# A graph network on one core: layer 1's weighted messages stay in their PSUM bank, and the sum scan and the first messages change places in the step

## The chip, the cores and the metric

One Trainium2 chip, one of its cores. The metric is the device time of one launch in microseconds (us). The kernel before took 4339.46 us, the median of 3 runs (4338.24 to 4342.36).

## What is computed

Two layers over a graph of 12500 nodes and 212500 edges, whose edges are sorted by destination. Each layer is followed by a residual sum and a layer norm. Layer 0 takes the maximum over a node's edges of a small network. The change lies in layer 1:

```python
x = h[src]; y = h[dst]
c = w_comp[etype]                                   # 16 coefficients per edge
xb = einsum('ei,bio->ebo', x, weight)
msg = einsum('eb,ebo->eo', c, xb)
x_hat = x @ A1_w.T + A1_b
y_hat = y @ A2_w.T + A2_b + rel_emb[etype]
a = tanh(relu(sum(x_hat * y_hat, -1) / sqrt(32)))
nei = segment_sum(a[:, None] * msg, dst)
```

`a * msg` are the weighted messages. A segmented scan along the sorted edges sums them, and the row of a node's last edge holds its sum.

## The kernel before, in words

The edges are cut into 4 streams, and each of 104 steps takes 512 edges of every stream: a tile is 128 partitions (4 streams by 32 features) by 512 edges. Every engine has its own program and works through it in order; semaphores tie them together. The order inside a step is written by hand in one function per engine, each called `step1` for layer 1. `run_steps` writes out the first 12 steps of layer 1, then a loop of 22 rounds with 4 steps each, then 4 more steps.

In step s of layer 1 the engines do the following.

- GpSimd (`gathers1`) fetches the source rows of step s+2 or so by indirect DMA, 128 rows per gather, at L691. Most steps need 15 gathers; the sixteenth tile is picked by matmuls with one-hot matrices (`hot_rows`, L1589). There are two buffers `xg`. A few gathers wait for `coef_done`.
- TensorE (`step1`, L1608) turns the gathered rows of the next step (`source_turn`, L1578 and, for the picked tile, L1575), forms 16 coefficient tiles (`coef`, L1513), each into one of the banks 2, 3 and 6 as `C_BANK` gives them, sums the score (`score_sum`, L1530), and adds up the messages in bank 7 in four parts (`messages`, L1522), of eight matmul records each. A coefficient waits until the product that read its bank before is done: `C_FREE[n]` is the number of products that must be. Coefficient 9 goes to bank 2, which coefficient 6 used before it, so `C_FREE[9]` is 7, products 0 to 6.
- VectorE (`step1`, L1300) multiplies each coefficient tile with the sources (`product`, L1254, eight buffers), and between the products it weighs the messages of the step before (`weigh`, L1262), scans them (`sum_scan`, L1269), scans the destination rows of the next step (`spread_scan`, L1138), adds and multiplies for the score (`find_query`, L1238; `find_score`, L1245), masks and adds the picked tile (L1285, L1293) and compares types (`one_hot`, L1189). Product 8 overwrites the buffer of product 0, so it waits for messages 0.
- ScalarE copies the turned sources (`x4_copy`, L874) and the composed coefficients out of PSUM, and forms the attention (`attend`, L879).
- SP's queue loads, in this order for a step: indices, types, spread rows, `keep` (waits for the scan four steps before) and the one-hot matrix (L573).

Before the change the weighted messages are the tile `wmsg`, a part of `hid` in SBUF. `weigh` reads bank 7 and writes it; `messages(s, 0)`, which overwrites bank 7, waits for `wmsg_ready`; `sum_scan` reads `wmsg` behind product 10.

Of the kernel before, what the change touches and what calls it, by code (L numbers as in the profile page):

```python
# [156 lines left out]
def build(nc, t):  # L157
    ctx = ExitStack()
    with ctx:
# [156 lines left out]
        h_cls = h.rearrange("p (c k) f -> p c (k f)", c=CLASSES)  # L316
        comp = sb("comp", [P, 2, 2, LEN], bf16)

        query, score, wmsg = (hid[:, k // 2, k % 2, :] for k in range(3))
        weight = xt  # L320
        node_t = hid[:, 1, 1, :]

        psum = ctx.enter_context(nc.psum_tensor("psum", [P, 8, 512], fp32))
        bank = [psum[:, i, :] for i in range(8)]
        hot_bank = [bank[6 + u][:, 0:PICK * F] for u in range(2)]
        hot_bank1 = bank[5][:, 0:PICK * F]
        lane_v = lane[:, 0:HOT_COLS].rearrange("p (s t) -> p s t", t=HOT)
# [602 lines left out]
        def _(dve):  # L930
# [365 lines left out]
            def products(s, a, b):  # L1296
                for n in range(a, b):
                    product(s, n)

            def step1(s):  # L1300
                behind, ahead, later = s.plus(-1), s.plus(1), s.plus(2)
                if has_pick(ahead):
                    mask_hot(ahead)
                product(s, 0)
                if has_pick(ahead):
                    add_hot(ahead)
                products(s, 1, 5)
                if behind.exists():
                    weigh(behind)
                products(s, 5, 7)  # L1310
                if ahead.exists():
                    spread_scan(1, ahead, 4)
                product(s, 7)
                if ahead.exists():
                    find_query(ahead)
                products(s, 8, 11)
                if behind.exists():
                    sum_scan(behind)
                products(s, 11, 14)
                if later.exists():  # L1320
                    one_hot(later)
                if has_pick(later):
                    find_lane(later)
                products(s, 14, 16)
                if ahead.exists():
                    find_score(ahead)
# [49 lines left out]
        def _(pe):  # L1376
# [139 lines left out]
            def messages(s, k):  # L1516

                wait_step(pe, s, prod_ready, each=SLOTS, more=(k + 1) * STREAMS - SLOTS)
                if k == 0:
                    wait_step(pe, s, wmsg_ready, lag=1)  # L1520
                for g in range(STREAMS):
                    last_ = pe.matmul(bank[7][F * g:F * g + F, :], basis[:, k, :],  # L1522
                                      prod[:, (k * STREAMS + g) % G_BUFS, :], start=k == 0, stop=k == KCH - 1,
# [84 lines left out]
            def step1(s):  # L1608
# [23 lines left out]
                coef(s, 8)  # L1632
                if turn:
                    source_turn(ahead, 2)
                messages(s, 0)
                coef(s, 9)
                if turn:
                    source_turn(ahead, 3)
                coef(s, 10)
                messages(s, 1)  # L1640
                if pick:
# [160 lines left out]
```

## Time and profile before

| | |
|---|---|
| median of 3 runs | 4339.46 us |
| the profiled execution | 4343.61 us |
| its span | 4341.8 us |
| its mean granted TensorE clock | 0.956 |
| TensorE matmul, busy | 3907.0 us |
| VectorE, busy | 3122.2 us |
| GpSimd, busy | 3217.8 us |
| ScalarE, busy | 903.0 us |

A profile is one execution. Its own time is a little over its span, the time from the first instruction to the last. A row of the timeline gives the start in us, the duration, the engine, the line, the operation, what is written and read, how many instructions follow one another, and in brackets how long the engine was idle before and what ended it. PE is TensorE, DVE is VectorE, POOL is GpSimd. Buffers share names: the products and the turned sources are parts of `late`, `wmsg`, the query and the score are parts of `hid`. Ends of matmuls are modelled.

### The profile page before, as it was taken

The numbers are of one execution on the slowest core, as the hardware profiler recorded it, in microseconds if no ns is written. First come the engines' busy times: TensorE is split into PE (matmuls) and PEld (weight loads), VectorE is DVE, ScalarE is ACT, GpSimd is POOL, SyncE is SP. The second block draws the span as 40 slices with busy tenths as digits, with TensorE's granted clock in tenths as the row PEclk, the third lists the DMA queues.
The fourth block names the chain that finished last, engine by engine and source line by source line (L and its number), as shares of the span: only waits on it lengthen the run. The fifth ranks groups of instructions, "written<-read, shape, count | busy, mean of one in ns | idle before, by whom it ended". The sixth has DMA issues, their size and how long they took to land.

```text
span 4341.8 us, 76892 instructions
## 1 busy us (share of the span) xinstructions
PE 3907.0 (90%) x23347; PEld 1771.7 (41%) x23347; DVE 3122.2 (72%) x5125; ACT 903.0 (21%) x1615; POOL 3217.8 (74%) x3330
## 2 busy tenths in 40 slices
PE   7989999999999999932989999999999999999941
PEld 3444554555455455411533333333333333333311
DVE  7856666666666666526678888888888888888844
ACT  4401111111111111110022222222222222222211
POOL 7767777777777777767777777777777777777745
PEclk9999999999999999965999999999999999999975
DMA  8123333333333333324145555555555555555511
GB/s 340 29 77 105 92 99 98 92 98 98 93 98 98 94 97 98 111 63 76 29 129 140 136 143 137 137 141 136 140 139 135 143 138 138 142 136 138 140 45 32
DMA packets 411406, 494.42 MB, mean 114 GB/s; under 512 B 165363, under 2 KB 314448, under 8 KB 409008
## 3 DMA queue, kind: packets, MB, share of 16 engines
q1 hardware_dynamic: 274800, 278.43, 25.1%
q0 software_dynamic: 106432, 131.97, 13.5%
q10 hardware_dynamic: 29952, 81.80, 5.0%
q14 instruction: 174, 1.43, 0.1%
q8 instruction: 48, 0.79, 0.1%
HBM read 345.09 MB, written 146.77 MB: 113 GB/s over the span
## 4 chain that ended last, share of the span: by engine, by line
PE 38%; DMA 8%; issue 5%; DVE 3%; POOL 1%; DVEq 0%; ACT 0%; POOLq 0%; ACTq 0%
PE psum L1589 8%; PE psum L1513 8%; PE psum L1522 8%; PE psum L1578 4%; DMA xg<-h_dram,src_idx 4%; PE psum L1676 3%; DMA last_rows<-sum_rows,last_i 2%; PE psum L1598 2%; DMA early<-max_rows,last_i 2%; PE psum L1551 1%; PE psum L1530 1%; DVE late L1254 1%; PE psum L1414 1%; PE psum L1575 1%; PE psum L1539 1%
## 5 line engine op out<-in xcount | busy, mean ns | idle before, releaser
L691 POOL DMA_INDIRECT xg<-h_dram,src_idx x1540 | 1502.7, 976 | 481.2 <-DMA xg<-h_dram,src_idx 345.3
L691 POOL DMA_INDIRECT xg<-in_x_dram,src_idx x1392 | 1328.7, 955 | 435.6 <-DMA xg<-in_x_dram,src_idx 306.4
L1254 DVE TENSOR_TENSOR late<-late,psum 128x512 f32<-128x512 f32 x1664 | 1080.0, 681 | 231.0 <-PE psum L1513 191.3
L1428 PE MATMUL psum<-early,late 128*128 128x448 bf16 x5712 | 1131.4, 354 | 9.5 <-DVE late L1051 7.4
L1428 PEld LDWEIGHTS psum<-early,late 128*128 128x128 bf16 x5712 | 545.0, 98 | 628.3 <-issue 115.9
L1513 PE MATMUL psum<-comp,sel 128*128 128x512 bf16 x1664 | 587.1, 384 | 42.1 <-DVE late L1254 41.5
L1522 PE MATMUL psum<-late,basis 128*32 128x512 f32 x3328 | 446.0, 608 | 0.0
L1589 PE MATMUL psum<-x,late 128*128 128x448 bf16 x1344 | 380.6, 353 | 0.0
L1051 DVE TENSOR_TENSOR late<-psum,lane_hot 128x448 f32<-128x448 f32 x272 | 169.7, 624 | 289.1 <-PE psum L1428 275.0
L1159 DVE TENSOR_TENSOR_SCAN scan<-fresh,scan,psum 128x512 f32<-128x512 bf16 x103 | 131.8, 1280 | 326.4 <-PE psum L1474 326.2
L1513 PEld LDWEIGHTS psum<-comp,sel 128*128 128x128 bf16 x1664 | 154.9, 98 | 493.5 <-DVE late L1254 299.3
L874 ACT COPY late<-psum 128x512 f32<-128x512 f32 x416 | 233.8, 587 | 520.8 <-PE psum L1578 307.1
L1032 DVE TENSOR_SCALAR late<-late,class_id 128x384 bf16<-128x384 f32 (+2 forms) x728 | 335.4, 531 | 0.0
L1138 DVE TENSOR_TENSOR_SCAN dt_<-keep,dt_,psum 128x512 f32<-128x512 bf16 x206 | 262.4, 1274 | 46.7 <-PE psum L1404 46.7
L1054 DVE TENSOR_REDUCE xg<-late 128x32 f32<-128x448 f32 x272 | 252.6, 929 | 9.3
L1578 PE MATMUL psum<-ident,xg 128*128 128x128 f32 x1540 | 229.8, 280 | 18.3 <-DMA xg<-h_dram,src_idx 12.8
L831 ACT ACTIVATE hid<-psum,b 128x512 f32<-128x512 f32 x208 | 131.6, 684 | 536.3 <-PE psum L1464 536.3
L1589 PE MATMUL psum<-late 128*128 128x448 bf16 x672 | 236.9, 352 | 0.0
L896 ACT COPY early<-psum 128x512 f32<-128x512 f32 x104 | 60.8, 585 | 822.4 <-PE psum L1414 822.4
L1494 PE MATMUL psum<-ident,early 128*128 128x128 f32 (+1 forms) x56 | 15.6, 434 | 231.1 <-DVE early L1180 119.5
L1578 PEld LDWEIGHTS psum<-ident,xg 128*128 128x128 f32 x1540 | 177.6, 142 | 97.6 <-ACT late L874 39.6
L836 ACT COPY out<-psum 128x512 f32<-128x512 f32 x104 | 61.0, 586 | 743.2 <-PE psum L1414 743.2
(159 smaller groups left out, 4424.7 us busy)
## 6 DMA issues: line engine op xcount, KB each, us to landing
sp_in<-spread SPq DMA_DIRECT2D x208, 256.0 KB, 3.7
late<-type_dram SPq DMA_DIRECT2D x104, 512.0 KB
sum_rows<-early ACTq DMA_DIRECT2D x104, 512.0 KB
spread<-late SPq DMA_DIRECT2D x16, 1664.0 KB
ea<-in_edge_t SPq DMA_DIRECT2D x104, 256.0 KB
keep<-keep_dram SPq DMA_DIRECT2D x832, 32.0 KB
max_rows<-out ACTq DMA_DIRECT2D x104, 256.0 KB, 2.1
xg<-h_dram,src_idx POOLq DMA_INDIRECT x1540
```

Of the source, the lines that this page charges most:

```text
L691: pool.indirect_dma_start(out=out, out_offset=None, in_=table, in_offset=bass.IndirectOffsetOnAxis(ap=index, axis=0), engine_sem=pool_issu ...
L874: act.copy(x4[:, s.slot(2), g, :], bank[g % 2][:, :]).then_inc(x_ready[1], 1)
L1032: last_ = dve.tensor_scalar(class_hot[u][:, tiles, c, :], class_in[:, u, tiles, :], class_id[:, c:c + 1], None, ALU.is_equal)
L1051: dve.tensor_tensor(picks[:, u], hot_bank[u].rearrange("p (h f) -> p h f", f=F), bc(lane_hot[:, t, :], size, 2), ALU.mult).then_inc(hot_re ...
L1054: dve.tensor_reduce(xg0[:, s.slot(PRE), SLOTS - hot_tiles(s) + t, :], picks[:, u].rearrange("p h f -> p f h"), AX.X, ALU.add).then_inc(hot ...
L1138: dve.tensor_tensor_scan(dt_[:, s.slot(2), :], keep[:, s.slot(4), :], bank[b][:, :], before(s, dt_), ALU.mult, ALU.add).then_inc(d_ready[n ...
L1254: dve.tensor_tensor(prod[:, n % G_BUFS, :], x4[:, s.slot(2), g, :], bank[C_BANK[n]][:, :], ALU.mult).then_inc(prod_ready, 1)
L1428: last_ = pe.matmul(hot_bank[tile_slot(s, t)], class_hot[s.slot(2)][:, HOT - hot_tiles(s) + t, c, :], x_parts[:, c, q, :], start=c == 0 an ...
L1513: pe.matmul(bank[C_BANK[n]][:, :], sel[:, (g % 2) * KCH + k, :], comp[:, s.slot(2), g // 2, :], start=True, stop=True).then_inc(coef_done, 1)
L1522: last_ = pe.matmul(bank[7][F * g:F * g + F, :], basis[:, k, :], prod[:, (k * STREAMS + g) % G_BUFS, :], start=k == 0, stop=k == KCH - 1, ...
L1578: last_ = pe.transpose(out[:, j, :], xg[:, s.slot(2), row, :], ident[:, :])
L1589: last_ = pe.matmul(hot_bank1, hot1[:, s.slot(2), c, :], h_parts[q][:, c, :], start=n == 0, stop=n == CLASSES * PARTS - 1)
```

## The change

`wmsg` becomes bank 7 itself. `weigh` reads bank 7 and writes its result over it, and the scan reads it there. The scan moves on VectorE from behind product 10 to behind product 5. The first messages of a step now wait for the scan of the step before in place of its `wmsg_ready`, and TensorE issues them behind coefficient 9 and the last source turn, where they stood behind coefficient 8 and turn 2.

```diff
--- before.py
+++ after.py
@@ -316,12 +316,13 @@
         h_cls = h.rearrange("p (c k) f -> p c (k f)", c=CLASSES)
         comp = sb("comp", [P, 2, 2, LEN], bf16)
 
-        query, score, wmsg = (hid[:, k // 2, k % 2, :] for k in range(3))
+        query, score = (hid[:, 0, k, :] for k in range(2))
         weight = xt
         node_t = hid[:, 1, 1, :]
 
         psum = ctx.enter_context(nc.psum_tensor("psum", [P, 8, 512], fp32))
         bank = [psum[:, i, :] for i in range(8)]
+        wmsg = bank[7]
         hot_bank = [bank[6 + u][:, 0:PICK * F] for u in range(2)]
         hot_bank1 = bank[5][:, 0:PICK * F]
         lane_v = lane[:, 0:HOT_COLS].rearrange("p (s t) -> p s t", t=HOT)
@@ -1307,16 +1308,16 @@
                 products(s, 1, 5)
                 if behind.exists():
                     weigh(behind)
-                products(s, 5, 7)
+                product(s, 5)
+                if behind.exists():
+                    sum_scan(behind)
+                product(s, 6)
                 if ahead.exists():
                     spread_scan(1, ahead, 4)
                 product(s, 7)
                 if ahead.exists():
                     find_query(ahead)
-                products(s, 8, 11)
-                if behind.exists():
-                    sum_scan(behind)
-                products(s, 11, 14)
+                products(s, 8, 14)
                 if later.exists():
                     one_hot(later)
                 if has_pick(later):
@@ -1517,7 +1518,7 @@
 
                 wait_step(pe, s, prod_ready, each=SLOTS, more=(k + 1) * STREAMS - SLOTS)
                 if k == 0:
-                    wait_step(pe, s, wmsg_ready, lag=1)
+                    wait_step(pe, s, scanned[1], lag=1)
                 for g in range(STREAMS):
                     last_ = pe.matmul(bank[7][F * g:F * g + F, :], basis[:, k, :],
                                       prod[:, (k * STREAMS + g) % G_BUFS, :], start=k == 0, stop=k == KCH - 1,
@@ -1632,10 +1633,10 @@
                 coef(s, 8)
                 if turn:
                     source_turn(ahead, 2)
-                messages(s, 0)
                 coef(s, 9)
                 if turn:
                     source_turn(ahead, 3)
+                messages(s, 0)
                 coef(s, 10)
                 messages(s, 1)
                 if pick:
```

## Rows read from the trace of the kernel before

**Rows 1.** The page, part 1: busy time, share of the span, instructions.

```profile
PE 3907.0 (90%) x23347; PEld 1771.7 (41%) x23347; DVE 3122.2 (72%) x5125; ACT 903.0 (21%) x1615; POOL 3217.8 (74%) x3330
```

**Rows 2.** Timeline of TensorE: start, duration, line, idle time before; two score sums.

```profile
2485.87 1.02 PE L1530 MATMUL psum<-hid,ones_blk 128*128 128x512 f32 x2
...
4104.77 1.02 PE L1530 MATMUL psum<-hid,ones_blk 128*128 128x512 f32 x2
```

**Rows 3.** Groups of instructions of GpSimd between the two starts of rows 2.

```profile
L691 POOL DMA_INDIRECT xg<-h_dram,src_idx x1261 | 1230.8, 976 | 389.4 <-DMA xg<-h_dram,src_idx 281.9 <-PE psum L1513 55.4 <-issue 52.0
```

**Rows 4.** Timeline around 2997 us, one gather and the scan it began in.

```profile
2997.33 1.28 DVE L1269 TENSOR_TENSOR_SCAN scan<-keep,scan,hid 128x512 f32<-128x512 bf16 x1
...
2997.55 1.82 POOL L691 DMA_INDIRECT xg<-h_dram,src_idx  x1 [0.30 <-DMA xg<-h_dram,src_idx]
```

**Rows 5.** Groups by form between 2200 and 4100 us, the two scans.

```profile
L1138 DVE TENSOR_TENSOR_SCAN dt_<-keep,dt_,psum 128x512 f32<-128x512 bf16 x99 | 125.9, 1272 | 0.0
L1269 DVE TENSOR_TENSOR_SCAN scan<-keep,scan,hid 128x512 f32<-128x512 bf16 x98 | 125.2, 1277 | 0.0
```

**Rows 6.** Timeline of TensorE in two successive steps.

```profile
3044.97 1.02 PE L1530 MATMUL psum<-hid,ones_blk 128*128 128x512 f32 x2
...
3050.19 1.04 PE L1578 MATMUL psum<-ident,xg 128*128 128x128 f32 x8
3051.07 0.38 PE L1513 MATMUL psum<-comp,sel 128*128 128x512 bf16 x1
3051.47 0.66 PE L1578 MATMUL psum<-ident,xg 128*128 128x128 f32 x4
3052.05 1.06 PE L1522 MATMUL psum<-late,basis 128*32 128x512 f32 x8
3053.05 0.39 PE L1513 MATMUL psum<-comp,sel 128*128 128x512 bf16 x1
3053.28 0.49 PE L1578 MATMUL psum<-ident,xg 128*128 128x128 f32 x3
...
3054.38 1.06 PE L1522 MATMUL psum<-late,basis 128*32 128x512 f32 x8
...
3063.64 1.02 PE L1530 MATMUL psum<-hid,ones_blk 128*128 128x512 f32 x2
...
3069.12 1.09 PE L1578 MATMUL psum<-ident,xg 128*128 128x128 f32 x8
```

**Rows 7.** Timeline of VectorE in the first of these steps.

```profile
3049.13 0.68 DVE L1262 SCALAR_TENSOR_TENSOR hid<-xt,psum 128x512 f32<-128x512 f32 x1
3049.73 1.28 DVE L1254 TENSOR_TENSOR late<-late,psum 128x512 f32<-128x512 f32 x2
3050.93 1.27 DVE L1138 TENSOR_TENSOR_SCAN dt_<-keep,dt_,psum 128x512 f32<-128x512 bf16 x1
3052.12 0.66 DVE L1254 TENSOR_TENSOR late<-late,psum 128x512 f32<-128x512 f32 x1
```

**Rows 8.** Timeline of the step before, at the loop's head, VectorE and TensorE.

```profile
3026.73 0.68 DVE L1254 TENSOR_TENSOR late<-late,psum 128x512 f32<-128x512 f32 x1
...
3027.46 0.39 PE L1513 MATMUL psum<-comp,sel 128*128 128x512 bf16 x1 [0.35 <-DVE late L1254]
...
3031.05 0.68 DVE L1262 SCALAR_TENSOR_TENSOR hid<-xt,psum 128x512 f32<-128x512 f32 x1
...
3035.71 1.07 PE L1522 MATMUL psum<-late,basis 128*32 128x512 f32 x8
```

**Rows 9.** Waits of VectorE: waited for, us in total, times, longest.

```profile
DVE late L1285 <- issue: 62.5, 21, 3.7
```

**Rows 10.** Timeline of TensorE, one long wait near each end of layer 1.

```profile
2261.58 1.93 PE L1578 MATMUL psum<-ident,xg 128*128 128x128 f32 x8 [2.65 <-DMA xg<-h_dram,src_idx]
...
4130.49 1.97 PE L1578 MATMUL psum<-ident,xg 128*128 128x128 f32 x8 [4.31 <-DMA xg<-h_dram,src_idx]
```

**Rows 11.** Busy time by stretch, 4130 to 4136 us; PEclk is third from the end.

```profile
4130.00:4136.00 6.00, 5.51 (x25) 3.17 (x26) 0.23 (x1) 1.76 (x3) 4.47 (x6) 0.53 0.23 51
```

## The prediction

> **What bounds the kernel now.** I began with the page. TensorE is busy for 90% of the span, VectorE for 72%, GpSimd for 74% [rows 1]. All lines of the diff lie in layer 1's loop, so I cut out its 84 like steps, from one score sum to another: 4104.77 - 2485.87 = 1618.9 us [rows 2]. Three engines run close together there, and the question is which of them is late at which point.
>
> GpSimd first. In that stretch it issues 1261 gathers, busy 1230.8 us and idle 389.4 us, together 1620.2 us, the whole stretch [rows 3]. The idle time is about 0.30 us behind each gather. It never rests: over many steps the gathers set today's rate, although TensorE looks fuller.
>
> Why do they take so long? The median gather takes 0.94 us, the mean 0.976 [rows 3]. One of the long ones, 1.82 us, began 0.22 us into the scan at L1269 and ended 0.76 us behind its end [rows 4]. I laid all gathers against all scans: 40 of those that began inside an L1269 scan were stretched so, and all of these ended 0.75 us or so behind it, 20.1 us in sum. Of 102 that began inside an L1138 scan none was. The two scans differ in one operand: L1138 reads its data from PSUM, L1269 from hid in SBUF [rows 5]. 15.3 of the 20.1 us lie in the 84 steps, 4.1 in the first 15 steps. The other stretched gathers overlap the one-hot at L1189, which stays.
>
> TensorE next. In a step where it waits for nothing, score sum to score sum takes 3063.64 - 3044.97 = 18.67 us; in the next, turn 0 starts 5.48 us into the step instead of 5.22, on the last gather [rows 6]. Of the 84 steps 27 are free like the first, 36 wait for a gather, and 21 stand at the loop's head, where VectorE stops for 3.0 us on average (62.5 us, 21 times, no releaser seen) [rows 9]. There TensorE follows VectorE for some coefficients.
>
> **The change, part by part.** I count from the score sum, t = 0 at 3044.97.
>
> *The scan's operand.* weigh and scan keep their number. The scan from PSUM takes 1272 ns against 1277 from SBUF [rows 5]: nothing on VectorE. On GpSimd it gives back the stretches, 15.3 us in the 84 steps, if something else doesn't bind. The Trainium skill speaks against it: VectorE: DVE Perf Modes, "The TRN2 errata", gives a fixed 120 cycles for a PSUM source against 58 for an SBUF one, that is 0.065 us more per scan, 5.5 us over 84 steps, by which the result would be near 4347. The trace does not agree (1272 against 1277 ns), and I go by the trace.
>
> *weigh writes PSUM, in the bank that it reads.* No VectorE row writes PSUM. Bounds: its successor starts 0.60 us behind it today, and the shortest row of 512 elements there lasts 0.66 us where weigh lasts 0.68, so 0.02 gained at most; at worst it costs what a scan does to its successor, 1.19 us, so 0.59 more [rows 7]. I take 0.60, the row of the same form.
>
> *The scan behind product 5.* VectorE reaches weigh at 4.16 and product 5 at 4.76 [rows 7]. Then the scan starts at 5.36 and product 6 at 5.36 + 1.19 = 6.55 (the pitch of L1138) and ends at 7.21 (0.66). Today it ends near 6.0. Queued behind the scan on VectorE are product 6, the spread scan, product 7, the query and products 8 to 10; then VectorE idles for coefficient 11 today, and that idle time takes up the shift, so the later ones don't move. What waits for product 6? Coefficient 9: they share bank 2 (C_FREE[9] = 7).
>
> *TensorE's order.* Today: turn 2 at 6.50, messages 0 at 7.08, coefficient 9 at 8.08, turn 3 at 8.31, messages 1 at 9.41 [rows 6]. A set of four transposes takes 0.44 us before a full-width coefficient (0.88 for the eight of turns 0 and 1), but 0.58 before messages. So TensorE would be ready for coefficient 9 at 6.50 + 0.44 = 6.94. It must wait for product 6 at 7.21, plus 0.06 for the semaphore (a product that ends at 3027.41 lets a coefficient go at 3027.46, others 0.06 to 0.07) [rows 8]: 7.27. From there turn 3 comes 0.23 later, then 1.10 as from turn 3 to messages 1 today, with 1.00 of messages 0 in between: messages 1 at 9.60 instead of 9.41. A free step costs **+0.19**, 18.86 us. Everything behind messages 1 keeps its place. Messages 0 start near 8.28; their new wait, the scan's end at 6.63, is covered, and product 8 at 9.5 finds them done at 9.28.
>
> *The loop's head.* There VectorE is late: weigh starts at 3031.05 and messages 1 at 3035.71 [rows 8]. By the same chain (0.60 + 0.60 + 1.19 + 0.66 + 0.06 + 2.33 = 5.44) messages 1 come at 3036.49: **+0.78**. Before, the lateness was over once messages 0 ran; now product 6 is behind a scan just where TensorE asks for it. Over the 21 heads, each from its own weigh, the mean is +0.70 (four with a short stop pay less).
>
> *The steps bound by gathers.* They fall to 18.86, which is 0.19 less on average, as GpSimd's need is then 1620.2 - 15.3 = 1604.9 us, below TensorE's.
>
> *Sum for the 84 steps:* 27 x 0.19 - 36 x 0.19 + 21 x 0.70 = 5.1 - 6.8 + 14.7 = **+13.0 us**, TensorE-bound at 1631.9.
>
> *Both ends of the layer.* In the first 15 steps GpSimd is last: TensorE waits 2.65 us at 2261.58 [rows 10] and short gather waits follow. Given back: the 4.1 us of stretches there, **-4.0**. At the other end TensorE waits 4.31 us at 4130.49 [rows 10], and then its granted clock is 0.53 for 6 us, between its two levels and mostly at 1.2 GHz [rows 11], which costs some 2.3 us. By then the gathers are 27 us less in arrears (1631.9 - 1604.9), as far as two xg buffers allow, over 10 us; both go: **-6.4**, with the longer step taken off.
>
> *SP, ACT.* SP's keep loads wait for the scan and go out 4.8 us earlier, then the hot load; their readers come steps later. ACT's copies for turns 2 and 3 end before these start. Nothing.
>
> **Total: +13.0 - 4.0 - 6.4 = +2.6 us.** The profiled execution took 4343.61 us (span 4341.8), the median of the runs 4339.46; the difference is between executions, so I put the sum on the median: **4342 us**. 0.2% of it, 8.7 us, is what a measurement can tell from no change.
>
> **Rivals.**
> *A, slower: writing weigh's result to its own PSUM bank costs time.* For it: no row shows that write. Against it: reads from PSUM cost nothing extra. The place is the chain weigh, product 5, scan, product 6, coefficient 9, which binds in all 84 steps, so each 0.1 us there is 8.4 us. It decides from (8.7 - 2.6) / 84 = 0.07 us up. With 0.15 us: 2.6 + 12.6 = +15, 4355; the upper bound, 0.59, would give 4392. Chance 0.22.
> *B, faster: product 6 is in time,* since the pieces around it are shorter than I have them, and coefficient 9 waits for nothing. TensorE then saves 0.14 a step (6.94 + 2.33 = 9.27), falls under the gathers' need, and the steps follow GpSimd: -15.3 - 4.0 = -19.3, 4320. For it: GpSimd is today's limit, and the change frees it. Against it: VectorE's pitches are read off rows, and 0.33 us is missing even in a free step, over 0.9 at the heads. The Trainium skill has a rule for B's first half: VectorE: DVE Perf Modes, "Two Vector instructions with no wait between them", says that the second of two SBUF tensor inputs is read through an interface shared with GpSimd. By that rule the trace agrees (40 stretched, 0 at L1138). Chance 0.16.
> *C, it does not do what it says:* gathers stretch as before, from whatever they collide with now that the SP loads are bunched, and absorb part of the waits at coefficient 9. Loop +13, ends nothing: with half absorbed +6.5, 4346. Chance 0.12, three quarters of it within 0.2%.
>
> **How the numbers follow.** The forecast has 0.50; its own spread is the stop at the loop's head (0.3 us a stop, 6 us in 21) and 0.05 us in the chain (4 us): 4334 to 4350. Of it 0.37 is within 0.2%, 0.10 slower, 0.03 faster. Slower: 0.10 + A 0.20 + C 0.03 = 0.33. Faster: 0.03 + B 0.16 = 0.19. Same: 0.37 + 0.02 + 0.09 = 0.48. The range takes in A's 4355 and the upper part of B: 4326 to 4356.
>
> **What would show it.** In the changed profile: the L1269 form's successor reads psum and lasts 1.27 us; no gather that begins in it is stretched; the mean gather falls from 976 to about 964 ns; coefficient 9 begins 7.27 us behind the score sum; free steps last 18.86; heads are 0.7 longer; GpSimd waits for TensorE at last; the 4.31 us wait near the end is gone. A weigh longer than 0.68, or product 5 over 0.60 behind it, speaks for A. Coefficient 9 at 6.94 and steps of about 18.7 to 18.9 bound by gathers speak for B. Stretched gathers inside the new scan speak for C, and if coefficient 9 still comes at 8.08, I have misread the order.

## The result and the profile after

The changed kernel takes **4303.11 us** (median of 4 runs, 4302.11 to 4305.04) where the kernel before takes 4339.51 in the runs beside it: ratio 0.9916, interval 0.9899 to 0.9933. It is 0.84% faster. I had forecast 4342 us, no change; the result lies outside the range, on the faster side.

All results below are ratios to the kernel before on the same chip, and this matters: on some chips the kernel before itself takes 5994 to 6053 us, on the others 4340 to 4346 us. Only the second kind behaves as the profiles of before and after do.

The page, part 1 (compare [rows 1]):

```profile
PE 3879.8 (90%) x23347; PEld 1782.7 (41%) x23347; DVE 3119.3 (73%) x5125; ACT 902.7 (21%) x1615; POOL 3183.5 (74%) x3330
```

GpSimd has 34 us less to do with the same instructions. The 84 steps, from score sum to score sum (compare [rows 2]), in TensorE's timeline:

```profile
2476.12 1.02 PE L1531 MATMUL psum<-hid,ones_blk 128*128 128x512 f32 x2
...
4072.32 1.02 PE L1531 MATMUL psum<-hid,ones_blk 128*128 128x512 f32 x2
```

That is 1596.2 us against 1618.9. The same stretch in the groups of instructions (compare [rows 3]):

```profile
L692 POOL DMA_INDIRECT xg<-h_dram,src_idx x1266 | 1205.5, 952 | 391.9 <-DMA xg<-h_dram,src_idx 282.9 <-issue 69.4 <-PE psum L1514 39.6
```

The mean gather fell from 976 to 952 ns. 1205.5 + 391.9 = 1597.4 us: GpSimd still hardly rests. VectorE's scan and GpSimd's gathers beside it (compare [rows 4, 5]):

```profile
3054.59 1.27 DVE L1270 TENSOR_TENSOR_SCAN scan<-keep,scan,psum 128x512 f32<-128x512 bf16 x1
3055.36 0.94 POOL L692 DMA_INDIRECT xg<-h_dram,src_idx  x1 [0.30 <-DMA xg<-h_dram,src_idx]
```

This gather begins 0.77 us into the scan and takes its 0.94 us. I call a gather well inside a scan when it begins at least 0.10 us behind the scan's start and at least 0.21 us before its end. In the changed kernel 68 gathers are well inside the moved scan and none is stretched; in the kernel before 41 were, and all 41 were stretched.

That is half of what GpSimd got back. Over the 84 steps, what the long gathers take beyond their usual 0.944 us adds up to 40.9 us in the kernel before: 15.3 in the scan, and 25.6 nearly all in gathers that overlap the one-hot of L1189, such as this one:

```profile
3058.68 1.27 POOL L691 DMA_INDIRECT xg<-h_dram,src_idx  x1 [0.31 <-PE psum L1513]
3059.08 0.75 DVE L1189 TENSOR_SCALAR late<-late,row_id 128x2048 bf16<-128x2048 bf16 x1
```

In the changed kernel the sum is 10.8 us, all of it outside the scan. So 15.3 us went with the operand and another 14.8 beside the one-hot, which was not touched: the gathers now meet it at other moments. The prediction had let these stand.

A plain step on TensorE (compare [rows 6]):

```profile
3049.23 1.02 PE L1531 MATMUL psum<-hid,ones_blk 128*128 128x512 f32 x2
...
3055.73 0.66 PE L1579 MATMUL psum<-ident,xg 128*128 128x128 f32 x4
3056.50 0.39 PE L1514 MATMUL psum<-comp,sel 128*128 128x512 bf16 x1
3056.72 0.49 PE L1579 MATMUL psum<-ident,xg 128*128 128x128 f32 x3
3057.14 0.43 PE L1576 MATMUL psum<-ident,xg 128*32 128x128 f32 x8
3057.39 1.04 PE L1523 MATMUL psum<-late,basis 128*32 128x512 f32 x8
3058.36 0.39 PE L1514 MATMUL psum<-comp,sel 128*128 128x512 bf16 x1
3058.68 1.06 PE L1523 MATMUL psum<-late,basis 128*32 128x512 f32 x8
...
3067.95 1.02 PE L1531 MATMUL psum<-hid,ones_blk 128*128 128x512 f32 x2
```

Coefficient 9 begins 7.27 us behind the score sum, as forecast. Messages 1 begin at 9.45, not 9.60, and the step takes 18.72 us, not 18.86. All 63 steps that are not the first of a round take 18.72; before, their mean was 18.89. VectorE in the same step (compare [rows 7]):

```profile
3053.39 0.69 DVE L1263 SCALAR_TENSOR_TENSOR psum<-xt,psum 128x512 f32<-128x512 f32 x1
3053.99 0.68 DVE L1255 TENSOR_TENSOR late<-late,psum 128x512 f32<-128x512 f32 x1
3054.59 1.27 DVE L1270 TENSOR_TENSOR_SCAN scan<-keep,scan,psum 128x512 f32<-128x512 bf16 x1
3055.78 0.66 DVE L1255 TENSOR_TENSOR late<-late,psum 128x512 f32<-128x512 f32 x1
3056.36 1.27 DVE L1139 TENSOR_TENSOR_SCAN dt_<-keep,dt_,psum 128x512 f32<-128x512 bf16 x1
```

`weigh`, which now writes PSUM, takes 0.69 us and its successor comes 0.60 behind it; product 6 begins at 6.55. This is the working of the prediction to the hundredth.

Another thing that I had not foreseen stands in VectorE's waits (compare [rows 9]; waited for, us in total, times, longest):

```profile
DVE late L1286 <- issue: 49.5, 21, 3.7
```

The stop at the head of a round fell from 2.98 to 2.36 us, and the head steps from 20.43 to 19.85 us, where I had 21.13. At both ends of the layer the waits of TensorE for gathers shrank: to 1.7 us in the first steps (2187 to 2486 us; 4.7 before), and to nothing in the last ones, where before it stood 4.31 us [rows 10].

Where the 39.8 us of the two spans lie:

| us | before | after | difference | forecast |
|---|---|---|---|---|
| start to the first score sum of layer 1 | 2191.8 | 2187.4 | -4.4 | 0 |
| the first 16 steps | 294.0 | 288.7 | -5.3 | -4.0 |
| 63 plain steps | 63 x 18.89 | 63 x 18.72 | -10.5 | |
| 21 head steps | 21 x 20.43 | 21 x 19.85 | -12.2 | |
| these 84 steps | 1618.9 | 1596.2 | -22.7 | +13.0 |
| the last three score sums | 60.0 | 51.8 | -8.2 | -6.4 |
| the rest | 177.0 | 177.9 | +0.9 | 0 |

The first row is no part of the change: over eight profiled executions on chips of this kind its time lies between 2187.0 and 2192.7 us, with no order in it.

### The profile page after: what moved, and what is told of

The parts are those of the page before. It is cut to its first block, busy times and chain, and to the rows that moved or that the text cites. A ratio compares the mean times of both kernels' runs of the same rounds, so it can differ in the third digit from the quotient of the medians.

```text
span 4302.0 us, 76892 instructions
## 1 busy us (share of the span) xinstructions
PE 3879.8 (90%) x23347; PEld 1782.7 (41%) x23347; DVE 3119.3 (73%) x5125; ACT 902.7 (21%) x1615; POOL 3183.5 (74%) x3330
## 4 chain that ended last, share of the span: by engine, by line
PE 30%; DVE 10%; issue 8%; DMA 5%; DVEq 1%; POOL 0%; ACT 0%; POOLq 0%; ACTq 0%
PE psum L1590 9%; PE psum L1523 6%; DVE late L1255 6%; PE psum L1514 6%; PE psum L1677 3%; DMA last_rows<-sum_rows,last_i 2%; PE psum L1599 2%; DMA early<-max_rows,last_i 2%; DVE psum L1263 1%; PE psum L1415 1%; DVEq L437 1%; PE psum L1579 1%; DVE xg L1294 1%; DMA xg<-h_dram,src_idx 1%; PE psum L1576 1%
## 5 line engine op out<-in xcount | busy, mean ns | idle before, releaser
L692 POOL DMA_INDIRECT xg<-h_dram,src_idx x1540 | 1466.5, 952 | 482.1 <-DMA xg<-h_dram,src_idx 346.0
L1255 DVE TENSOR_TENSOR late<-late,psum 128x512 f32<-128x512 f32 x1664 | 1085.8, 680 | 213.6 <-PE psum L1514 202.0
L1052 DVE TENSOR_TENSOR late<-psum,lane_hot 128x448 f32<-128x448 f32 x272 | 169.9, 625 | 286.8 <-PE psum L1429 273.0
L1139 DVE TENSOR_TENSOR_SCAN dt_<-keep,dt_,psum 128x512 f32<-128x512 bf16 x206 | 262.5, 1274 | 45.8 <-PE psum L1405 45.8
L1495 PE MATMUL psum<-ident,early 128*128 128x128 f32 (+1 forms) x56 | 15.6, 435 | 232.2 <-DVE early L1181 119.9
```

The costliest lines, as they stand in the source:

```text
L692: pool.indirect_dma_start(out=out, out_offset=None, in_=table, in_offset=bass.IndirectOffsetOnAxis(ap=index, axis=0), engine_sem=pool_issu ...
L1052: dve.tensor_tensor(picks[:, u], hot_bank[u].rearrange("p (h f) -> p h f", f=F), bc(lane_hot[:, t, :], size, 2), ALU.mult).then_inc(hot_re ...
L1139: dve.tensor_tensor_scan(dt_[:, s.slot(2), :], keep[:, s.slot(4), :], bank[b][:, :], before(s, dt_), ALU.mult, ALU.add).then_inc(d_ready[n ...
L1255: dve.tensor_tensor(prod[:, n % G_BUFS, :], x4[:, s.slot(2), g, :], bank[C_BANK[n]][:, :], ALU.mult).then_inc(prod_ready, 1)
```

## The experiments

There were two theories. **G**: the scan's operand in SBUF stretches the gathers, they set the rate, and the place of the messages (PSUM) makes the gain. **R**: the two new orders make it. Later a third question came up: what sets the stop at the head of a round.

### Both orders, messages in SBUF (e13)

```diff
-        query, score = (hid[:, 0, k, :] for k in range(2))
+        query, score, wmsg = (hid[:, k // 2, k % 2, :] for k in range(3))
...
-        wmsg = bank[7]
...
-                    wait_step(pe, s, scanned[1], lag=1)
+                    wait_step(pe, s, wmsg_ready, lag=1)
```

> Both new orders, the weighted messages in SBUF, the ordinary data. On a chip of some 4340 us: theory R (the two orders make the gain; e12 kept TensorE's 18.72 us a plain step with 25 of 87 gathers inside the scan stretched) expects the changed kernel's ratio, 0.990 to 0.993, plain steps of 18.72 us and a head step of 19.7 to 20.1. Theory G (the place of the messages makes it, through the gathers) expects 0.996 or more and plain steps over 18.8 us. On a chip of some 6000 us both expect 0.992 to 0.995, as in e8.

Measured: 4319.1 us, ratio 0.9948 (0.9931 to 0.9965), between the two theories. So the orders are worth 0.5% and the place, on top of them, about 0.3% (the two intervals just touch, but this kernel's fastest run, 4316.9 us, lies above the changed kernel's slowest, 4305.0); by the spans 22.7 us (4341.8 to 4319.1, of which 4.8 lie ahead of layer 1) and 17.1 (to 4302.0). A gather in GpSimd's timeline, and TensorE's waits from 2440 to 4040 us:

```profile
3098.41 1.84 POOL L691 DMA_INDIRECT xg<-h_dram,src_idx  x1 [0.30 <-DMA xg<-h_dram,src_idx]
```

```profile
PE psum L1513 <- DVE late L1254: 27.3, 51, 1.1
PE psum L1578 <- DMA xg<-h_dram,src_idx: 1.5, 2, 0.8
```

31 gathers are stretched in the scan again, by 19.0 us in sum, among them all 28 that are well inside it; with the place moved to PSUM (the changed kernel) it is 0 of 68. G's mechanism is shown. But in the 84 steps the stretches hardly bind: TensorE waits 1.5 us for gathers and its plain steps take 18.73 us. The reason is again in GpSimd's rows: over the 84 steps the long gathers lose 12.1 us in the scan, little less than the 15.3 before, but 5.2 us outside it, where it was 25.6. So part of what the orders gain comes through the gathers too, by the one-hot and not by the scan. Stretch by stretch, the place is worth 5.0 us of the 84 steps (1601.2 against 1596.2), 5.7 of the first 16 (294.4 against 288.7) and 7.8 of the last three (59.6 against 51.8). The orders are worth 17.7 us in the 84 steps, and within 0.4 us nothing in the first 16 and the last three.

### Messages in PSUM, TensorE's old order (e14)

```diff
                 if turn:
                     source_turn(ahead, 2)
+                messages(s, 0)
                 coef(s, 9)
                 if turn:
                     source_turn(ahead, 3)
-                messages(s, 0)
```

> Messages in PSUM, the scan early, messages 0 ahead of coefficient 9 as before. From e13 (both orders with SBUF: 0.9948) the place is worth 0.4% and the orders 0.5%. If TensorE's own move gives the orders' part, by sparing product 6's semaphore a wait, this kernel has plain steps of 18.8 to 19.0 us and a ratio of 0.995 to 1.000. If the move is neutral or costs 0.19 us a step, as my prediction had it, plain steps are 18.6 us or less and the ratio is 0.989 to 0.991.

Measured: 4314.19 us (4302.88 to 4315.70), ratio 0.9926 (0.9910 to 0.9943), in neither of the two ranges expected, the interval overlapping the changed kernel's. The profiled execution is the fastest, 4302.88. Messages 0, turn 3 and messages 1 in a plain step, from the score sum at 3049.10:

```profile
3056.18 1.06 PE L1523 MATMUL psum<-late,basis 128*32 128x512 f32 x8
3057.40 0.49 PE L1579 MATMUL psum<-ident,xg 128*128 128x128 f32 x3 [0.16 <-issue]
3057.82 0.43 PE L1576 MATMUL psum<-ident,xg 128*32 128x128 f32 x8
3058.50 1.07 PE L1523 MATMUL psum<-late,basis 128*32 128x512 f32 x8
```

Messages 1 at 9.40 and 18.67 us a plain step, against 9.45 and 18.72. TensorE's own move therefore costs 0.05 us a step, as a mechanism of the sign that I had forecast and a quarter of its size. It brings no gain in this profile: the 84 steps take 1594.3 us, the least of the kernels with a stop at the head. Whether it pays in the runs at 4313 to 4316 us stays open; I have no profile of one.

### TensorE's order alone (e15)

```diff
-                messages(s, 0)
                 coef(s, 9)
                 if turn:
                     source_turn(ahead, 3)
+                messages(s, 0)
```

> Messages in SBUF, the scan behind product 10 as before, messages 0 behind coefficient 9. Gathers under the scan: if the early scan's place among the gathers is what lets them run ahead, the lead stays at 5 gathers as before, over 35 are stretched inside the scan, and the ratio is 0.998 to 1.003. If TensorE's order alone makes the orders' part, 0.994 to 0.996.

Measured: 4365.75 us, ratio 1.0044 (1.0027 to 1.0060): slower than before, just outside the first expectation and far from the second. TensorE's waits, 2440 to 4040 us, and GpSimd's group there:

```profile
PE psum L1578 <- DMA xg<-h_dram,src_idx: 45.7, 54, 1.0
```

```profile
L691 POOL DMA_INDIRECT xg<-h_dram,src_idx x1230 | 1225.6, 996 | 375.8 <-DMA xg<-h_dram,src_idx 275.1 <-issue 72.6 <-PE psum L1513 28.1
```

All 97 gathers well inside the scan are stretched, by 66.7 us; the mean gather takes 996 ns and the plain steps 19.33 us. With the scan at its old place the engines have settled so that a gather begins 0.1 to 0.5 us into nearly every scan. That is the gathers' rate in its pure form: over the 84 steps the gathers lose 22.9 us more than in the kernel before (63.8 against 40.9), and the steps take 21.5 us more. TensorE's move alone costs time; VectorE's move pays in e14 without it, together with PSUM. VectorE's move by itself, with the messages in SBUF, has no run on these chips.

### The changed kernel with VectorE's instructions moved in memory (e16)

```diff
+            for _ in range(64):
+                dve.wait_ge(dve_done, 1)
             run_steps(dve, step1, 4, 3)
```

> The changed kernel with 64 fulfilled waits ahead of VectorE's steps of layer 1, so that every instruction of the steps lies elsewhere in memory. If the layout of the 8 KB pieces sets the heads (e11 and e12, with other instructions ahead of the steps, had heads of 20.9 us at the same stop of 2.0 us): the head steps move off 19.85 us by 0.5 us or more and the time by 10 us or more either way. If only the gathers' lead and the DMAs that meet the loads set them: head steps of 19.6 to 20.1 us and the time within 0.15% of 4303 us.

Measured: 4305.74 us, ratio 0.9904 (0.9888 to 0.9921). VectorE's waits, the line that takes the place of the stop, and TensorE's:

```profile
DVE late L1255 <- remote: 15.0, 21, 0.8
```

```profile
PE psum L1581 <- DMA xg<-h_dram,src_idx: 16.6, 43, 0.9
```

The stop is gone from in front of L1286; 0.7 us of it are left, 21 times, in front of a product. So half of each expectation came true: the head steps moved, by 1.0 us to 18.86, and the time did not. The DMA queue q14, which carries instructions, shows why the stop went: in the 84 steps it moves 117 packets of 8192 bytes in the kernel before, in the changed one and in e11 to e15, and 13 here. The 64 waits took away five loads a round, so those were VectorE's. Yet the time did not move, because now TensorE waits for gathers: the 84 steps take 1586.5 us, 9.7 less, which is 15 gathers of 0.950 and their 0.31 us of idle time (18.9 us) a step; the last three steps pay 6.4 us for gathers that are no longer ahead (58.2 against 51.8), the first 16 pay 3.4, and 3.5 lie ahead of layer 1. **With gathers of this length 1586 us is what GpSimd allows, whatever is done to the heads.**

### The same with layer 0's result set to zero (e11, e12)

```diff
                 link(dve.reciprocal(stat_c[:, :], stat_b[:, :]))
+                if n < CHUNKS:
+                    link(dve.memset(stat_c[:, :], 0.0))
```

e12 has e13's edit too. Both were meant for the chips of 6000 us, and met one of 4342.

> The changed kernel with layer 0's result h set to zero (one memset on VectorE a chunk, in front of layer 1): every gather, one-hot row, product, turn and scan of layer 1 runs as before, on zeros. It asks why the kernel took about 6000 us on the chips of the first three jobs, where TensorE stood some 6 us in each step. Theory P (TensorE is held there for what its data make it draw): on such a chip the 84 steps of layer 1 fall from 28.7 us towards the 19 us of the first profiles, 104 steps by up to 1000 us, and layer 0's steps stay. Theory Q (it is held for its activity, whatever the data, or for its instructions): the time stays within 1% of the changed kernel's. On a chip that takes 4340 us for the kernel before, both expect 4303 us within 5 us.

> The same zeros with both new orders and the weighted messages in SBUF. If the zeros bring the steps of 19 us back (or the chip has them anyway): theory G (the scan's SBUF operand stretches GpSimd's gathers, and they set the rate) expects 0.3% or more over e11 (13 us or more), over 30 stretched gathers inside the scan, and TensorE waiting for gathers in several steps; theory R (the two orders make the whole gain) expects e11's time within 0.15%. If the steps stay at 28 us, both expect no difference, as in e7 and e8.

Measured: 4474.8 us (ratio 1.0305, 1.0288 to 1.0322) and 4474.8 us (1.0311, 1.0293 to 1.0328). Neither theory had that. The plain steps take 18.72 us in both, although in e12 all 25 gathers well inside the scan are stretched, which bears e13 out; the head steps take 28.0 and 26.7. VectorE's waits in e11 (2440 to 4200 us), GpSimd's, and one head:

```profile
DVE late L1288 <- issue: 146.5, 21, 8.6
DVE xg L1296 <- issue: 47.1, 21, 6.3
```

```profile
POOL xg L692 <- ACT early L892: 182.1, 30, 11.1
```

```profile
3050.85 0.75 DVE L1248 SCALAR_TENSOR_TENSOR hid<-psum,a1b,hid 128x512 f32<-128x512 f32 x1
3059.53 0.62 DVE L1288 TENSOR_TENSOR late<-psum,lane_hot 128x448 f32<-128x448 f32 x1 [7.93 <-issue]
```

The extra memsets move VectorE's instructions as e16's waits do, and here it costs: there is a second stop in each round, in front of L1296, of 1.1 us in the second and third head and about 2 us or more in the others. Those two heads take 20.9 us at a first stop of 2.3. The gathers get further ahead with each round, and from the fifth head on, when GpSimd is a whole step ahead and stands for the buffers, the first stop is 7.4 to 8.6 us. That gave the clue to what the stop is.

### What the stop is: DMA packets in front of the instruction load

VectorE's instructions come in DMA packets of 8192 bytes on queue q14 (e16). At each head of a round VectorE goes on 2.0 to 2.4 us behind the start of one such load, in all 105 heads of before, after, e13, e14 and e15 and in the 42 of e11 and e12, however long it stands. The DMA view of the 4 us before a head, in the kernel before (3019.4 to 3023.4 us; packets, MB, share of 16 engines):

```profile
q1 hardware_dynamic: 432, 0.51, 43.6%
q0 software_dynamic: 230, 0.48, 40.6%
q14 instruction: 1, 0.01, 1.0%
```

and in the changed one (3005.3 to 3009.3 us):

```profile
q0 software_dynamic: 127, 0.26, 23.5%
q1 hardware_dynamic: 22, 0.03, 2.2%
```

q1 carries SP's loads. SP's issues before the head at 3023.38 us in the kernel before:

```profile
3011.48 0.35 SPq L654 DMA_DIRECT2D src_idx<-in_src_t  x1
3012.09 0.38 SPq L656 DMA_DIRECT2D late<-type_dram  x1
...
3017.77 1.85 SPq L579 DMA_DIRECT2D keep<-keep_dram  x4
3019.99 0.35 SPq L573 DMA_DIRECT2D late<-hot_dram  x1
```

and before the head at 3009.18 us in the changed one:

```profile
2992.60 0.35 SPq L655 DMA_DIRECT2D src_idx<-in_src_t  x1
2993.20 0.38 SPq L657 DMA_DIRECT2D late<-type_dram  x1
...
2998.76 2.98 SPq L580 DMA_DIRECT2D keep<-keep_dram  x4
3002.12 0.35 SPq L574 DMA_DIRECT2D late<-hot_dram  x1
```

The `keep` load waits for a scan, and the scan is 5.1 us earlier (it starts 5.36 us behind the score sum, where it started 10.42 behind, both medians); the index and type loads wait for gathers, and the gathers are further ahead. So the whole burst goes out earlier and ends earlier. Means over the 21 heads, in us relative to the end of `find_score`, after which VectorE stands (a minus is before it). The burst on q1 ends with the last packet of the run that begins with the one-hot load; "ahead" is how many gathers have begun at a typical head's score sum, counted from 5 in the kernel before:

| kernel | type load issued | one-hot load issued | burst on q1 ends | load before the head's | head's load starts | stop | ahead |
|---|---|---|---|---|---|---|---|
| before | -11.3 | -3.4 | +0.5 | -2.4 | +0.7 | 2.98 | 5 |
| e15, late scan | -11.1 | -2.4 | +0.6 | -2.2 | +0.6 | 2.88 | 5 |
| e13, early scan | -12.4 | -5.4 | -0.6 | -2.8 | +0.4 | 2.53 | 7 |
| e14, early scan | -13.9 | -6.5 | -1.8 | -4.0 | +0.2 | 2.38 | 8 |
| after | -15.6 | -7.2 | -3.0 | -4.2 | +0.2 | 2.36 | 9 |

Over the 105 heads of these five kernels the head's load never starts less than 2.6 us behind the load before it. Where that one starts 3.5 us or more before the end of `find_score` (34 heads, on average 177 DMA packets that start within 3 us of that point) the mean stop is 2.2 us; where it starts within 2.2 us (21 heads, 675 packets) it is 3.4 us. VectorE's new program by itself doesn't make the stop short: in the changed kernel the first and third head, where the bursts still run over the head (to +1.9 and +0.7), have stops of 3.7 and 3.5 us.

The plainest case is in e11 and e12. At 31 of their heads the type load, 512 packets of 1024 bytes, goes out at -2.1 to -1.9 us and runs over the head. The head's load starts at +5.3 to +6.5, and in 30 of the 31 within 0.3 us of the end of the type load's last packet. At the fourth head of e11 the type load goes out at +0.5, behind the start of the head's load, and that stop is 2.1 us; the second stop is the one of 6.3. That traffic holds the load back is shown there. That it does so in the kernel before as well, and that the earlier loads are what shortened the stop from 2.98 to 2.36, is read from timing, head by head; I tried no kernel in which SP's loads alone are held back.

The Trainium skill has the frame for this: Runtime: NRT & Kernel Launch, "Instruction fetch mechanics", says that a sequencer fetches its instructions through a DMA queue of its own, and that a taken branch whose target is not in its window must wait for the fetch. The trace agrees with the second part, 1.9 to 8.6 us a head. On the size, 16 KiB a block by the Trainium skill, VectorE's loads disagree, with 8192 bytes each; the 48 loads on q8, none of them in the loop, are of 16384.

### The chips of 6000 us (e1 to e10, e17, e18)

On these the kernel before takes 5994 to 6053 us. The changed kernel there, the page's part 1 and two rows of VectorE's waits:

```profile
PE 4286.2 (71%) x23079; PEld 1885.4 (31%) x23347; DVE 3143.2 (52%) x5125; ACT 906.2 (15%) x1615; POOL 3170.3 (53%) x3330
```

```profile
DVE late L1255 <- remote: 606.8, 188, 9.3
DVE late L1052 <- remote: 543.2, 88, 17.3
```

VectorE's, ScalarE's and GpSimd's busy times are within 1% of those on the other chips, but VectorE, ScalarE and GpSimd wait, up to 17 us at a time, for releases that the profile puts down to nothing on the core, in layer 0 (L1052) as in layer 1 (L1255); TensorE's granted clock is 0.856 and the steps take 28.7 us. I did not find out why. The edits: e1 and e5 are e13's kernel, e8 too; e2 is e15's; e4, e9 and e18 are e14's; e7 is the changed kernel, e10 is e16's; e6 and e17 are the kernel before with e16's 64 waits; e3 is the kernel before with VectorE's move alone:

```diff
-                products(s, 5, 7)
+                product(s, 5)
+                if behind.exists():
+                    sum_scan(behind)
+                product(s, 6)
...
-                products(s, 8, 11)
-                if behind.exists():
-                    sum_scan(behind)
-                products(s, 11, 14)
+                products(s, 8, 14)
```

> Both moves of the change, but wmsg stays in hid in SBUF and the first messages wait for wmsg_ready as before. Theory G (the scan's SBUF operand stretches gathers, and the gathers set the rate): stretched gathers inside the scan come back, about 40 or more, the mean gather rises to 970 ns or more, the time is 4325 to 4350 us. Theory R (the gain is TensorE's and VectorE's order, the operand does little): 4303 to 4310 us with coefficient 9 at 7.27 us and a plain step of 18.72. For the shorter stop at the loop's head (2.35 us mean in place of 2.98): if it comes from VectorE's order of instructions it stays at 2.3 to 2.5; if it comes from the gathers being ahead it goes back to 2.9 to 3.1.

> Only TensorE's order changes: messages 0 behind coefficient 9 and turn 3. Product 6 is in time then, so coefficient 9 should begin near 6.94 us into a plain step and messages 1 near 9.12, a step of 18.39 us if nothing else binds. Theory G: the gathers set the rate, so the time stays at 4337 to 4342 us. Theory R: 84 steps gain 0.28 each, 4312 to 4318 us. Head stop: 2.9 to 3.1 if VectorE's order sets it, since that order is the old one.

> Only VectorE's order changes: the scan behind product 5, from SBUF, TensorE's order as before. Coefficient 9 comes behind messages 0 at 8.08, where product 6 is long done, so a plain step keeps 18.67. Theory G: stretched gathers as before or more, 4335 to 4350 us. Theory R: the heads alone gain, 4318 to 4325 us. Head stop: 2.3 to 2.5 if VectorE's order sets it, 2.9 to 3.1 if not.

> The change without its TensorE part: in place in PSUM, scan behind product 5, messages 0 behind coefficient 8 and turn 2 as before. A plain step goes from 18.72 back to 18.67 (coefficient 9 at 8.08, no wait for product 6), 63 x -0.05 = -3; at a head messages 0 may wait up to 0.2 us for the scan, but coefficient 9 no longer waits for product 6 (-0.5 to -0.8 a head). Theory G with TensorE as the bound of the changed kernel: 4288 to 4302 us, TensorE's move worth nothing or a loss. If TensorE's move was needed for the gain, 4305 us or more.

> The kernel of e1 once more, since before itself took 6050 us in that job. Theory G (the scan's SBUF operand stretches gathers and the gathers set the rate): with the median of before near 4340 us this one takes 4325 to 4350 us, with 40 or more stretched gathers inside the scan. Theory R (the two orders make the gain): 4303 to 4312 us. Head stop 2.3 to 2.5 us if VectorE's order of instructions or the place of the scan sets it, 2.9 to 3.1 if the gathers' lead does.

> The kernel before with 64 waits that are long fulfilled, once, ahead of VectorE's layer 1 steps: nothing in the loop changes, but its instructions lie elsewhere in memory and in the 8 KB pieces in which the instruction queue loads them. Theory L (where the pieces' borders fall decides how late the load at the loop's head starts): the mean stop at the 21 heads leaves 2.98 us by 0.3 or more and the time moves by 5 to 25 us, either way. Rival (the stop hangs on traffic or on the order inside the loop): stop 2.9 to 3.1, time within 3 us of before.

> The changed kernel itself, beside the runs of before on the same chip. On a chip like that of the first profiles: ratio 0.992. On one where the kernel before takes about 6000 us, as in the two jobs so far: theory R (the new orders of VectorE and TensorE make the gain) expects the ratio of the run with both orders and the messages in SBUF, 0.990 to 0.994; theory G (the SBUF operand stretches GpSimd's gathers and those set the rate) expects clearly less, about 0.985.

> Both new orders, the weighted messages in SBUF as before. Theory R (orders make the gain): within 0.2% of the changed kernel, 0.990 to 0.994 of before. Theory G (the stretched gathers set the rate): at most half of the gain is left, 0.996 or more where the changed kernel has 0.992; over 30 of some 100 gathers inside the scan are stretched again, and TensorE waits for gathers again where it does not in the changed kernel.

> The weighted messages in PSUM and VectorE's new order, but messages 0 ahead of coefficient 9 on TensorE as before. Beside the slow chips (1.022): if TensorE's move is what makes the early scan pay, at least 0.5% slower than the changed kernel on any chip. If on TensorE's ordinary clock the move is worth nothing, as my prediction's term of +0.19 us a step has it, this kernel is as fast as the changed one or up to 0.4% faster (84 steps by 0.19 us are 16 us).

> The changed kernel with 64 waits that are always fulfilled ahead of VectorE's steps of layer 1: they move every later instruction of VectorE by a constant in memory and leave each step as it is. Theory L (where the 8 KB pieces of instructions end sets the stop at the head of a loop): the mean stop at the 21 heads moves off 2.35 us, by 0.3 us or more, and the time by 7 us or more (0.2%). Theory O (the shorter stop comes of the order inside the loop or of gathers that are ahead): the stop stays within 0.2 us and the time within 0.15%.

> The kernel before with the same 64 fulfilled waits: by e16 VectorE should then find its instructions at the head of a loop, and the stop of 2.98 us a head be gone. Theory L (the stops, 21 of them, cost before what after does not pay): the 84 steps fall by the heads' excess, 21 x (20.43 - 18.89) = 32 us, and the kernel is as fast as the changed one. Theory G (the gathers set the rate in the kernel before, whatever the heads do): the steps lose their heads but the plain ones grow, TensorE waits for gathers more than 8.8 us, over 60 gathers inside the scan are stretched, and at most 12 us are gained (ratio 0.997 or more).

> The kernel of e14 again; its runs lay at 4302.9 and at 4313 to 4316 us. Its plain steps of 18.67 us against 18.72 say that TensorE's move costs 0.05 us a step, some 3 us, where the engine sets the rate. If the runs at 4313 to 4316 us are this kernel's usual ones, a profile of one of them shows the 11 us in other steps than the plain ones: at the heads, in steps 4 to 14 or in the last three. If the move is worth nothing, the median is within 0.1% of the changed kernel's 4303 us.

| kernel | ratio there | ratio on the other chips |
|---|---|---|
| changed (e7) | 0.9940 (0.9923 to 0.9956) | 0.9916 |
| changed, moved in memory (e10) | 0.9949 (0.9932 to 0.9965) | 0.9904 |
| both orders, SBUF (e1, e5, e8) | 0.9938, 0.9902, 0.9940 | 0.9948 |
| TensorE's order alone (e2) | 1.0034 (1.0016 to 1.0052) | 1.0044 |
| PSUM, TensorE's old order (e4, e9, e18) | 1.0222, 1.0169, 1.0198 | 0.9926 |
| VectorE's order alone (e3) | 1.0200 (1.0180 to 1.0219) | not run |
| before, moved in memory (e6, e17) | 1.0005, 1.0006 | not run |

What follows: there the place is worth nothing once the scan is early (e7 and e8 are equal, and in neither does a gather begin inside the scan), and the early scan pays only together with TensorE's move (e3 and e4 against e1 and e7), which on the ordinary chip costs 0.05 us a step. Both findings belong to that regime. e10 and e6 asked about a stop that is not what limits there: the 64 waits take the loads away there too (13 packets on q14 in the 84 steps where e7 has 118), and the time stays. e17 was to tell whether the kernel before is set by its gathers even without the stops; it met such a chip, and that stays open.

## Why the prediction was wrong

**What held.** The bound: GpSimd never rests in the kernel before, and the gathers that are stretched in the scan come of its SBUF operand; without the operand there are none (0 of 68; e13 brings them back, e15 shows them setting the rate). The scan from PSUM costs VectorE nothing: 1274 ns against 1277. The errata rule of the Trainium skill (VectorE: DVE Perf Modes, "The TRN2 errata"), by which each scan should have cost 0.065 us more, an estimate from its cycle counts, is not borne out, as [rows 5] had said. The write to `weigh`'s own bank is free (0.69 us against 0.68, and its successor 0.60 behind it as before), so rival A falls. Coefficient 9 waits for product 6 and starts at 7.27, so rival B's mechanism falls too, though its direction was right. Rival C falls with the first point. The start gave 5.3 us for 4.0 forecast, the end 8.2 for 6.4; e13 assigns 5.7 and 7.8 of them to the place.

**What failed, first: "SP's keep loads wait for the scan and go out 4.8 us earlier ... Nothing."** They did go out earlier, and as far as the timing tells that was worth most. I asked only whether the readers of the loads would notice. The burst in which they travel had been ending just where VectorE fetches instructions for a round, and now it ends 3.4 us sooner. I had the stop as a constant of 3.0 us with a spread of 0.3; it is a wait for a DMA (e16), other traffic lengthens it (e11), and the change moved the traffic. The mean stop fell to 2.36 us.

**Second, the term "21 x 0.70".** It took the stops as they were. At an equal stop the price was right: the changed kernel's heads with stops of 3.7 and 3.5 us take 21.5 and 21.7, the kernel before's with 3.7, 3.6 and 3.5 take 20.9, 20.9 and 21.0, so 0.6 to 0.8 more, where I had 0.78 for the head of [rows 8]. But at 2.4 us the price is 0.1 (19.8 against 19.7). The stops shrank into the range where VectorE has caught up before coefficient 9. Together these make 21 x (21.13 - 19.85) = 26.9 us of the error.

**Third, a term mis-sized: the free step.** +0.19 was forecast, +0.05 measured, 18.67 to 18.72 (e14 against the changed kernel). I placed messages 0 near 8.28 by the pitches of the old order; right behind the last source turn they start at 8.16, coefficient 10 comes 0.97 behind them instead of 1.00, and messages 1 follow at 9.45. 63 x 0.14 = 8.8 us.

The heads and the free steps make 35.7 us in the 84 steps, which is +13.0 - (-22.7). The other 6.7 us are the ends (3.1) and the stretches in which nothing was changed (3.5).

**Fourth, a premise of the whole sum: the one-hot's stretches, "which stays".** They fell from 25.6 to 10.8 us in the 84 steps, so the mean gather came to 952 ns where I had 964, and GpSimd's need sank by 30 us and not by 15.3. This is no further term of the error, but the others could not have come without it: at the need that I had forecast for GpSimd, 1604.9 us, the steps could not take 1596.2.

**Open.** A gather well inside a scan with the SBUF operand is stretched always: 41 of 41 in the kernel before, 28 of 28 in e13, 97 of 97 in e15. How many there are is a matter of where gathers begin. In e13 most of the others begin in the scan's first 0.1 us or its last, and nearly all of those take their 0.94 us. What sets these moments I can only report. Whether the kernel before would gain without its stops was not settled, nor what VectorE's move is worth alone, nor TensorE's on an ordinary chip beyond its 0.05 us.

## What to carry to other kernels

A stop with no releaser at the head of a loop can be an instruction load, as it was here: look at what travels on the other queues in the 5 us before it, and count every transfer that a moved instruction releases as moved too, for the traffic and not for its reader alone. Price a term at the stops that the changed kernel will have, and where two engines are within 1% of each other, expect that what one gives back the other takes: in e16 the heads gave 21 us more, the plain steps took 11 of them back for the gathers, and both ends the rest.

## What the hardware showed that I had not expected

- VectorE's instruction load at the head of a round costs 1.9 to 4.0 us in before, after, e13, e14 and e15, and up to 8.6 us when a load of 512 packets of 1024 bytes is under way (e11), whose end it then waits for; 64 waits of no effect, ahead of the loop, took it away, with five of the 5.6 loads a round (e16).
- A gather that begins well inside a scan with its data in SBUF ends 0.75 us behind the scan, every time (166 of 166 in before, e13 and e15); with the data in PSUM it is never stretched (0 of 149 in after, e14 and e16).
- Engines that run at nearly the same pace lock: in e15 97 of 104 scans had a gather begin well inside them, in the kernel before 41, with the same instructions on VectorE and GpSimd.
- The same program takes 4340 us on one chip and 6050 us on another, with nearly equal busy times on VectorE, ScalarE and GpSimd, and a change that gains 0.7% on the one (e14) loses 2% on the other.
